# A Mamba mixer inside a decoder kernel: decays from running sums, single-activation silus, and a new order of the stages

## What is computed

```
zxBCdt = x @ in_proj_w.T                  # 512 z, 512 xc, 8 step sizes, 64 C, 64 B
dt = softplus(Bm + dt_bias)               # per token and head, 8 heads
xc = silu(depthwise_causal_conv(xc, conv_w, conv_b))        # 4 taps
a_bar = exp(dt * A)                       # A = -exp(A_log)
h = a_bar * h + b * x;  y_t = h . c       # a scan over the 256 tokens
y = (y + xh * D) * silu(z)
out = rms_norm(y, norm_w) @ out_proj_w.T
x1 = layernorm(x + out)
```

## Time and profile before

| | |
|---|---|
| median of 3 runs | 2436.24 us (2429.4 to 2440.71) |
| the profiled execution's own time | 2424.99 us |
| its span, first to last instruction | 2423.2 us |
| PE busy in the span | 2191.4 us (90%) |
| PEld | 1910.5 us (79%) |
| DVE | 1790.1 us (74%) |
| ACT | 1396.7 us (58%) |
| POOL | 1258.2 us (52%) |

### The profile page before, as it was taken

How to read it: one execution, slowest core, us unless ns; L and a number is a source line. 1 busy time by engine, 2 the same in 40 slices (tenths; PEclk the granted TensorE clock), 3 DMA queues, 4 the chain that set the end, 5 groups by cost and what they waited for, 6 DMA issues and landing times. The chain is left out here.

```text
span 2423.2 us, 53605 instructions
## 1 busy us (share of the span) xinstructions
PE 2191.4 (90%) x15804; PEld 1910.5 (79%) x15805; DVE 1790.1 (74%) x4428; ACT 1396.7 (58%) x3046; POOL 1258.2 (52%) x1411
## 2 busy tenths in 40 slices
PE   6999999999997897999999999999958999999776
PEld 5777777777775786888888888888848999999733
DVE  7888888888886424676777777677746777777778
ACT  5565565655653424666666666666626665556533
POOL 4677676776765001343434344343435776667755
PEclk9999999999998898999999999999979999999955
DMA  4011011110100453222222222222246877777588
GB/s 146 27 31 39 26 39 35 30 39 26 39 30 22 164 201 101 80 93 84 94 77 82 91 78 82 79 95 77 75 156 203 254 242 220 242 226 238 174 291 269
DMA packets 185263, 278.49 MB, mean 115 GB/s; under 512 B 26076, under 2 KB 107492, under 8 KB 185188
## 3 DMA queue, kind: packets, MB, share of 16 engines
q1 hardware_dynamic: 171140, 240.84, 31.8%
q0 software_dynamic: 12960, 35.67, 4.1%
q10 hardware_dynamic: 1088, 1.07, 0.1%
HBM read 184.13 MB, written 93.38 MB: 115 GB/s over the span
## 5 line engine op out<-in xcount | busy, mean ns | idle before, releaser
L1439 ACT ACTIVATE b_wk_f<-b_ps_s,b_nmx 128x77 f32<-128x77 f32 x1024 | 234.6, 347 | 15.4 <-DVE b_nmx L1487 15.4
L570 DVE SCALAR_TENSOR_TENSOR a_conv<-a_xc_pad,a_cw,a_conv 128x256 f32<-128x256 f32 x384 | 237.2, 677 | 8.4 <-ACT a_conv L457 8.4
L1447 ACT ACTIVATE b_pT<-b_ps_pT 77x1024 f32<-77x1024 f32 x128 | 130.7, 1021 | 142.3 <-PE b_ps_pT L1345 142.3
L2054 POOL DMA_INDIRECT made_scratch<-c_o_s,c_to x142 | 147.8, 1041 | 86.4 <-issue 42.4
L112 PE MATMUL c_ps_h<-c_xT_hi,c_w 128*128 128x256 f32 x568 | 168.0, 296 | 26.6 <-DMA c_b_c<-in_c_b 20.6
L1926 ACT ACTIVATE c_hid<-c_ps_h,c_b_c 128x256 f32<-128x256 f32 x284 | 111.6, 476 | 134.4 <-issue 76.0
L1503 DVE TENSOR_TENSOR b_oT_lo<-b_ps_oT,b_oT_hi 128x512 fp32r<-128x512 f32 x128 | 88.0, 687 | 130.6 <-ACT b_oT_hi L1453 130.6
L1732 POOL CAST w<-b_w_raw 128x256 f32 (+1 forms) x32 | 13.6, 425 | 323.9 <-DMA b_w_raw<-in_c_w 323.9
L1430 ACT ACTIVATE b_qT<-b_ps_q,b_bq_s 128x256 f32<-128x256 f32 x256 | 107.7, 473 | 112.4 <-PE b_ps_q L114 109.6
L1970 DVE TENSOR_TENSOR c_h_lo<-c_hid,c_h_hi 128x1024 fp32r<-128x1024 f32 x71 | 97.5, 1373 | 91.5 <-ACT c_h_hi L1935 60.9
L112 PE MATMUL c_ps_o<-w,c_h_hi 128*128 x568 | 160.0, 282 | 3.5 <-DVE c_h_lo L1970 3.5
(11 more groups left out here) (271 smaller groups left out, 7858.8 us busy)
## 6 DMA issues: line engine op xcount, KB each, us to landing
c_w<-parts_scratch SPq DMA_DIRECT2D x71, 1024.0 KB
c_xa<-sent_scratch SPq DMA_DIRECT2D x71, 260.0 KB, 2.9
d_got<-made_scratch SPq DMA_DIRECT2D x32, 512.0 KB, 5.4
keys_scratch<-k_k_s SPq DMA_DIRECT2D x8, 1232.0 KB, 4.8
b_kz<-keys_scratch SPq DMA_DIRECT2D x64, 154.0 KB, 2.8
b_vv<-values_scratch SPq DMA_DIRECT2D x32, 308.0 KB
a_xT_f<-in_xT SPq DMA_DIRECT2D x32, 256.0 KB, 3.1
a_x_f<-in_x SPq DMA_DIRECT2D x32, 256.0 KB, 2.7
```

Of the source, the lines that this page charges most:

```text
L570: dve.scalar_tensor_tensor(out=conv[:, m, :], in0=xc_pad[:, m, k:k + L], scalar=cw[:, m, k:k + 1], in1=conv[:, m, :], op0=ALU.mult, op1=AL ...
L1439: last = act.activation(pe_[:, u.par, c, :], s_scores[:, c // (C // GM), c % (C // GM), :], ACT.Exp, bias=nmx[:, u.par, c:c + 1])
L1447: act.activation(pT[:, u.par, :, :], ps_pT[0:LK, :, :], ACT.Copy).then_inc(s_pTc, 1)
L2054: pool.indirect_dma_start(routing.made, bass.IndirectOffsetOnAxis(to[:, t.slot, c:c + 1], 0), o_s[:, t.par, c, :], None).then_inc(s_sent[t ...
```

## The change

All of it is in `mixer_phase`.

- The decays' exponents are no longer sums over a masked matrix. The new stage cumulate makes running sums of the log decays, in one fp32 product of 64 rows by 128 columns. cum_high (ScalarE) and cum_parts (VectorE) split them in a high and a low part, cum_parts writes 32 rows of a_to_s, and spread_cum (GpSimd) writes 32 rows of a_to_t. decay(c) multiplies a_to_s by a_to_t, 128 rows in fp32r. Other rows hold constants made once in prep_decay on VectorE (some ten instructions) from one more load, mk_pair.
- z and conv are turned into silu by one Silu activation each; the two tanh activations and VectorE's gate and silu_conv are gone. x_high moves from VectorE to ScalarE.
- weigh also clamps a_e_x to at most 1, in the same instruction.
- The order of the lists changes on all four engines. On TensorE in_z and step_size come after decay(1), and out between decay(0) and decay(1). mix_off waits for the first instruction of bias_dt of the next sequence, cumulate for a_l_dt.

Cut to what matters:

```diff
-        conv_t = sb("conv_t", [P, MI, L])
-        z_t = sb("z_t", [P, NT, DI])
-        l_dt = sb("l_dt", [P, 2, NT * H])
-        lm = sb("lm", [P, NT, H, P])
+        l_dt = sb("l_dt", [P, 2, 4, NT * H])
+        cum_hi = sb("cum_hi", [4 * NT * H, P], F32R)
+        cum = sb("cum", [4 * NT * H, P], F32R)
+        to_t = sb("to_t", [P, H, P], F32R)
+        to_s = sb("to_s", [P, NT, P], F32R)
...
+            sp.dma_start(mk_pair[P // 2:P, :, :, :], masks.rearrange("(k w) m t -> k w m t", w=2)).then_inc(s_load, 16)
...
+            def cumulate(b):
...
+                pe.wait_ge(s_l, b.count(1, 1))
+                if not b.before(1):
+                    pe.wait_ge(s_or, b.ago(1).count(1, 1))
+                pe.matmul(ps_cum, l_dt[:, b.par, :, :].rearrange("p r n -> p (r n)"), upto, start=True, stop=True
+                          ).then_inc(s_cum, 1)
...
-                        last = pe.matmul(p23[:, j, :], after,
-                                         lm[:, c, 4 * j:4 * j + 4, :].rearrange("p h t -> p (h t)"),
+                        last = pe.matmul(p23[:, j, :], to_s[:, c, :],
+                                         to_t[:, 4 * j:4 * j + 4, :].rearrange("p h t -> p (h t)"),
...
             def mix_off(b):
...
+                if not (b.known() and b.value() == n_seq - 1):
+                    pe.wait_ge(s_v, b.ago(-1).count(1, 1))
...
-                (in_x, 0), (turn_y, 2), (in_z, 0), (in_bc, 0), (step_size, 0), (scores, 1), (decay(0), 1), (turn_x, 1),
-                (decay(1), 1), (out, 2), (mix, 1), (mix_off, 1)])
+                (in_x, 0), (cumulate, 1), (turn_y, 2), (turn_x, 1), (in_bc, 0), (scores, 1), (decay(0), 1),
+                (out, 2), (decay(1), 1), (in_z, 0), (step_size, 0), (mix, 1), (mix_off, 1)])
...
-                act.activation(z_t[:, :, :], p45[:, :, :], ACT.Tanh, scale=0.5).then_inc(s_zt, 1)
+                act.activation(zs[:, b.par, :, :], p45[:, :, :], ACT.Silu).then_inc(s_zs, 1)
...
-                act.activation(conv_t[:, :, :], conv[:, :, :], ACT.Tanh, scale=0.5).then_inc(s_ct, 1)
+                act.activation(sx[:, b.par, :, :], conv[:, :, :], ACT.Silu).then_inc(s_sx, 1)
+
+            def x_high(b):
...
+                act.activation(xT_hi[:, b.par, :, :], xT_f[:, b.par, :, :], ACT.Copy).then_inc(s_xhi, 1)
+
+            def cum_high(b):
...
+                act.activation(cum_hi[:, :], ps_cum, ACT.Copy).then_inc(s_chi, 1)
...
-                (take_xc, 0), (squares, 2), (y_high, 2), (tanh_z, 0), (take_bc, 0), (exp_decay(0), 1), (exp_rc, 1),
-                (take_x, 1), (exp_decay(1), 1), (tanh_conv, 0), (softplus, 0)])
+                (cum_high, 1), (x_high_next, 0), (y_high, 2), (take_xc, 0), (take_bc, 0), (exp_rc, 1),
+                (exp_decay(0), 1), (take_x, 1), (squares, 2), (exp_decay(1), 1), (silu_z, 0), (silu_conv, 0),
+                (softplus, 0)], spare=2)
...
-                    dve.tensor_tensor(mt[:, c, :, :], e_x[:, c, :, :],
-                                      g_m[:, 2 * c, :].unsqueeze(1).to_broadcast([P, H, P]), ALU.mult
-                                      ).then_inc(s_mt, 1)
+                    dve.scalar_tensor_tensor(out=mt[:, c, :, :], in0=e_x[:, c, :, :], scalar=1.0,
+                                             in1=g_m[:, 2 * c, :].unsqueeze(1).to_broadcast([P, H, P]),
+                                             op0=ALU.min, op1=ALU.mult).then_inc(s_mt, 1)
...
+                dve.tensor_tensor(l_dt[:, b.par, :, :], v_sp[:, :].unsqueeze(1).to_broadcast([P, 4, NT * H]),
+                                  a_rep[:, :].unsqueeze(1).to_broadcast([P, 4, NT * H]), ALU.mult).then_inc(s_l, 1)
+
+            def cum_parts(b):
...
+                dve.scalar_tensor_tensor(out=cum[:, :], in0=ps_cum, scalar=of_part[:, 1:2],
+                                         in1=cum_hi[:, :].bitcast(F32), op0=ALU.mult, op1=ALU.subtract
+                                         ).then_inc(s_wn, 1)
...
+                dve.tensor_tensor(to_s[32:64, :, :], cum[32:64, :].bitcast(F32).unsqueeze(1).to_broadcast([32, NT, P]),
+                                  to_s_sel[32:64, :].unsqueeze(2).to_broadcast([32, NT, P]), ALU.mult
+                                  ).then_inc(s_to_s, 1)
...
-                (prep_once, 0), (x_high_next, 0), (taps(0, 1), 0), (y_low, 2), (gate, 0), (bias_dt, 0), (mask_g, 1),
-                (taps(1, 2), 0), (weigh(0), 1), (weigh(1), 1), (taps(2, 3), 0), (normalise, 3), (add_d, 1),
-                (silu_conv, 0), (log_decay, 0), (residual, 2)], spare=2)
+                (cum_parts, 1), (y_low, 2), (mask_g, 1), (normalise, 3), (taps(0, 1), 0), (weigh(0), 1),
+                (taps(1, 2), 0), (weigh(1), 1), (taps(2, 3), 0), (bias_dt, 0), (add_d, 1), (prep_once, 0),
+                (residual, 2), (log_decay, 0)], spare=2)
...
-                for c in range(NT):
-                    last = pool.tensor_tensor(lm[:, c, :, :],
-                                              l_dt[:, b.par, H * c:H * c + H].unsqueeze(2).to_broadcast([P, H, P]),
-                                              upto.unsqueeze(1).to_broadcast([P, H, P]), ALU.mult)
-                last.then_inc(s_lm, 1)
+                pool.tensor_tensor(to_t[0:32, :, :], cum[0:32, :].bitcast(F32).unsqueeze(1).to_broadcast([32, H, P]),
+                                   to_t_sel[0:32, :].unsqueeze(2).to_broadcast([32, H, P]), ALU.mult).then_inc(s_lm, 1)
...
-                (x_low_next, 0), (inv_rms, 2), (scale_x, 1), (join, 1), (spread_l, 0), (inv_std, 2)], spare=2)
+                (x_low_next, 0), (spread_cum, 1), (inv_rms, 2), (scale_x, 1), (join, 1), (inv_std, 2)], spare=2)
```

More of the change, by code:

```diff
@@ L445, in _, with x_high_next @@
             act.activation(a_neg[:, :], a_neg[:, :], ACT.Exp).then_inc(s_whi_a, 1)
+            def x_high_next(b):
+                if not (b.known() and b.value() + 1 >= n_seq):
+                    x_high(b.ago(-1))
             def take_xc(b):
@@ L553, in prep_out @@
                                   ).then_inc(s_wout, 1)
-            def x_high(b):
-                dve.wait_ge(s_xT_in[b.par], b.half * 16 + 16)
-                if not b.before(2):
-                    dve.wait_ge(s_bc, b.ago(2).count(1, 1))
-                dve.tensor_copy(xT_hi[:, b.par, :, :], xT_f[:, b.par, :, :]).then_inc(s_xhi, 1)
             def taps(first, end):
@@ L573, in taps @@
                 return run
-            def gate(b):
-                dve.wait_ge(s_zt, b.count(1, 1))
-                if not b.before(2):
-                    dve.wait_ge(s_y, b.ago(2).count(NT, NT))
-                dve.scalar_tensor_tensor(out=zs[:, b.par, :, :], in0=z_t[:, :, :], scalar=1.0, in1=p45[:, :, :],
-                                         op0=ALU.add, op1=ALU.mult).then_inc(s_zs, 1)
             def y_low(b):
@@ L688, in _, with prep_decay @@
                                   ).then_inc(s_wprep, 1)
-            def x_high_next(b):
-                if not (b.known() and b.value() + 1 >= n_seq):
-                    x_high(b.ago(-1))
+            def prep_decay():
+                rows = ident[0:4 * NT * H, 0:4 * NT * H]
+                dve.tensor_reduce(of_head[:, :], rows.rearrange("p (j h) -> p h j", h=H), AX.X, ALU.add
+                                  ).then_inc(s_sel, 1)
+                dve.tensor_reduce(of_block[:, :], rows.rearrange("p (g c h) -> p c g h", c=NT, h=H), AX.XY, ALU.add
+                                  ).then_inc(s_sel, 1)
+                dve.tensor_reduce(of_part[:, :], rows.rearrange("p (u w f) -> p w u f", u=2, w=2), AX.XY, ALU.add
+                                  ).then_inc(s_sel, 1)
+                dve.wait_ge(s_sel, 3)
+                dve.tensor_scalar(sign[:, :], of_part[:, 1:2], 2.0, -1.0, ALU.mult, ALU.add).then_inc(s_sel, 1)
+                dve.tensor_copy(to_s[0:32, :, :], of_block[0:32, :].unsqueeze(2).to_broadcast([32, NT, P])
+                                ).then_inc(s_sel, 1)
+                dve.tensor_copy(to_t[32:64, :, :], of_head[32:64, :].unsqueeze(2).to_broadcast([32, H, P])
+                                ).then_inc(s_sel, 1)
+                half = slice(P // 2, P)
+                dve.tensor_tensor(to_s[half, :, :], mk_pair[half, 0, 2, :].unsqueeze(1).to_broadcast([P // 2, NT, P]),
+                                  mk_pair[half, 1, 2, :].unsqueeze(1).to_broadcast([P // 2, NT, P]), ALU.add
+                                  ).then_inc(s_sel, 1)
+                dve.tensor_scalar(to_t[half, :, :], mk_pair[half, 0, 1, :].unsqueeze(1).to_broadcast([P // 2, H, P]),
+                                  NEVER, None, ALU.mult).then_inc(s_sel, 1)
+                dve.wait_ge(s_sel, 8)
+                dve.tensor_scalar(to_t_sel[:, :], of_head[:, :], sign[:, 0:1], None, ALU.mult).then_inc(s_sel, 1)
+                dve.tensor_scalar(to_s_sel[:, :], of_block[:, :], sign[:, 0:1], -1.0, ALU.mult, ALU.mult
+                                  ).then_inc(s_sel, 1)
             def prep_once(b):
```

116 lines of the change are left out of this document (69 added, 47 removed).

## The result

| | before | after |
|---|---|---|
| median of 7 runs each | 2436.24 us (2429.4 to 2448.76) | 2414.64 us (2409.85 to 2425.32) |
| ratio, 95% interval | | 0.9926 [0.9902, 0.9951] |
| the profiled execution's own time | 2424.99 us | 2424.2 us |

What follows compares the result with a forecast made beforehand. TensorE's work plus about 1.8 us of waits bounds the 23.43 us mixer period; the new order gives 22.6. 29 x 0.83 = 24 us, plus some 2 at the end, takes the median from 2436 to 2410 us, range 2356 to 2446.

Steps and rivals of the forecast that it cites:

- The chain: One mixer period from cumulate through ScalarE's activations and squares, scalings and taps, mix_off and log decays: 22.6 us.
- The turns: After ScalarE's second a_e_x, VectorE's weigh(1) and taps alternate with GpSimd's scalings: 5.8 us, to 17.25.
- The wait before mix_off: On TensorE, mix_off waits for bias_dt behind VectorE's taps: released at 17.35 with TensorE free at 16.4, about 1 us.
- Table loads: On ScalarE, four activation table loads per step, each 1.28 us, with no further drain.
- the rival that made it 2.67: ScalarE table switches cost 2.67 us each: period 26.0 us, +75 us, 2511 us; chance 0.02.
- The clock: Slower rival: TensorE's mixer clock falls through idling, mean 0.83, period 24.1 us, +20 us, 2456 us; chance 0.07.
- my own sign: In the changed profile, a mixer granted clock other than 1.00 would show the main step wrong.
- The last steps: At the mixer's end, spread_l and the decays are hidden by nothing, so the change gains some 2 us.
- The first steps: At the mixer's start, prep_decay and one more load cost 2 to 3 us, which cheaper decays give back: even.
- The turns cost little: Rival: GpSimd's three scalings fit VectorE's gaps, taps end at 14.2, period 20.6 us, 84 us gained, 2352 us; chance 0.22.
- Even: Rival: one more hold-up of 0.8 us on the single chain eats the gain, period 23.4 us, 2434 us; chance 0.13.
- The decays stay slow: Rival: TensorE's fp32r decays are as slow as before, period 23.8 us, +9 us, 2445 us; chance 0.03.

Runs made afterwards that it cites:

- the extra products: Changed kernel plus five unread 512-column products in TensorE's waits before cumulate and decay(0): 2398.06 us; with only the two before decay(0): 2400.37 us.

## Why the prediction was right, point by point

**The steps of one period at full clock**, from the start of cumulate at 306.69, as forecast and as measured:

| | forecast | measured |
|---|---|---|
| turn_y done, next starts | 1.25 | 1.29 |
| decay(0) starts | 4.8 | 4.87 |
| squares done | 10.5 | 10.64 |
| inv_rms done | 11.6 | 11.96 |
| the taps done | 17.25 | 16.75 |
| mix_off waited | about 1 | 0.16 |
| mix_off ends | 18.45 | 18.08 |
| the sum on GpSimd ends | 20.75 | 20.27 |
| next cumulate | 22.6 | 22.04 (22.24 in another) |

The chain is the one forecast, and its costs hold: 0.37 us from cumulate to turn_y (0.4), pairs of decays 0.64 to 0.73, a_to_t 1.89 (1.97), Silu 1.02 to 1.06 (1.02), four loads of 1.28.

- **The turns** between VectorE and GpSimd were right in kind and 0.5 us too dear. I added up both sides' work, 5.8 us; it was done in 5.17, from 318.27 to 323.44, so about a tenth of it ran side by side. The Trainium skill, in "SBUF — State Buffer", section Who interferes with whom, says that a VectorE instruction with two SBUF inputs contends with a GpSimd instruction that reads SBUF. The trace agrees: four taps take 4.03 us beside GpSimd, and 1.66 with GpSimd idle.
- **The wait before mix_off** was to cost TensorE about 1 us. It was 0.16: the taps ended 0.5 earlier, and TensorE was free at 16.8, not 16.4.
- **Table loads.** That a switch costs 1.28 us and no more held for all four, and the rival that made it 2.67 is gone: its 26.0 us period is nowhere. The Trainium skill's "ScalarE: Activation LUTs", What ACT_TABLE_LOAD costs, gives 1.283 us for the load, as here, and some 1.38 of drain beside it. The trace doesn't show the drain: a_zs at 319.55 stands 0.02 behind the end of the load of 318.25.
- **The clock** is where I was wrong, and it was given 0.07. Step by step: "1.56 in every period leaves the clock at 1.00, and my longest wait is 1.3" took the longest wait as what counts, and by my own sign (a granted clock that isn't 1.00) that step was wrong. The clock came down in 19 of 29 periods, over the output projection, though no wait was longer than 1.21 us. Filling the 0.9 to 1.2 us before cumulate left 15 falls; filling the 0.4 to 0.7 before decay(0) left one. The same two waits with fp32 decays left two. So the length of the longest wait says little; the place and the work around it count, and by which rule is not shown. It fell less than the rival needed for a slower kernel: 10 periods at 1.00 and 19 at 0.93 are a mean of 0.954, and that rival decides under 0.9.
- **Errors that nearly cancel.** (716.20 - 56.42) / 29 = 22.75 us is the mean period, against 22.6. At full clock it was 22.17, 0.43 under the forecast, which is 12 us over 29 periods; the falls add 0.58 each, 17 us. With the extra products in place the time was 2398 to 2400: without the falls, the forecast would have been 11 us too high, not 5 too low. That it came within 5 us is in part luck.
- **The rest of the sum.** Taken from turn_y to turn_y, the 29 periods are 21.0 us shorter (680.4 to 659.4), against 24. The last steps gain 1.5, against 2. The first steps, which I took as even, lose 6.9: the first turn_y starts at 57.13 instead of 50.25. Of these, 3.0 are there when in_x starts (14.10 instead of 11.15), since GpSimd's first x_low waits for the added load, mk_pair. The others come with a wait of 7.33 us before the first cumulate and a granted clock of 0.59 to 0.73 between 30 and 50 us, where it was 0.74 to 1.00. Together that is the 15.6 us of the mixer; the medians show 6 more, inside the spread of the phases behind it.
- **The rivals.** "The turns cost little" wanted 20.6 and is out: no kernel's periods came under 21.2. "Even" was one hold-up of 0.8 us away; as a sum it was nearly right for two periods in three (23.07), by another cause. "The decays stay slow" was run as an experiment: 23.5 where I wrote 23.8, and 2441 where I wrote 2445.
- **Not asked in the forecast:** which edit carries the gain. Silu alone gives all of it, fp32r alone most of it, in the old order the two add up to 38 us. The new order with its running sums gains 16 to 21 us less than that; how much of it is the order, the running sums, the first steps or the clock wasn't parted.
